# Graph network on one Trainium2 core: the aggregation passes gather each edge tile once instead of once per step

## What is computed

```python
def _sage_layer(h, edge_src, edge_dst, W, b, inv_deg):
    msgs = h[edge_src]
    agg = jax.ops.segment_sum(msgs, edge_dst, num_segments=h.shape[0]) * inv_deg
    y = jnp.concatenate([h, agg], axis=1)
    return y @ W + b
h = jnp.maximum(_layernorm(x, axis=-1), 0.0)
x = x + _L0_gnn_ref(h, src, dst, ...)     # two sage layers, relu between, log_softmax
h = jnp.maximum(_layernorm(x, axis=-1), 0.0)
x = x + _L1_gnn_ref(h, edge_index, edge_weight1, ...)   # two transformer convolutions
```

## Time and profile before

| | |
|---|---|
| median of 3 runs | 9773.23 us (9768.02 to 9782.53) |
| the profiled execution | 9781.53 us |
| its span from first to last instruction | 9779.8 us |
| GpSimd busy | 6426.5 us (66%) |
| VectorE busy | 5351.2 us (55%) |
| TensorE busy (matmul) | 5061.4 us (52%) |
| TensorE weight loads | 4259.1 us (44%) |
| ScalarE busy | 2964.1 us (30%) |
| line 537, first pass | 1664 gathers, 1595.2 us busy |
| line 537, second pass | 1664 gathers, 1581.2 us busy |
| line 1150, gathers of the convolution | 3328, 3187.6 us busy |

### The profile page before, as it was taken

How to read it: one execution, slowest core, us unless ns; L and a number is a source line. 1 busy time by engine, 2 the same in 40 slices (tenths; PEclk the granted TensorE clock), 3 DMA queues, 4 the chain that set the end, 5 groups by cost and what they waited for, 6 DMA issues and landing times. The chain is left out here.

```text
span 9779.8 us, 124105 instructions
## 1 busy us (share of the span) xinstructions
PE 5061.4 (52%) x23048; PEld 4259.1 (44%) x23048; DVE 5351.2 (55%) x14932; ACT 2964.1 (30%) x6482; POOL 6426.5 (66%) x6729
## 2 busy tenths in 40 slices
PE   1444444446544444443256666666655666666665
PEld 1333333335433333333145555555524555555553
DVE  5333333332333333333767777777766777777776
ACT  2000000001000000000236666666533666666653
POOL 4777777772577777776057777777605777777760
PEclk8555555557655555555677777777777777777777
DMA  5222222222222222222355555555435555555543
GB/s 119 53 53 53 53 53 53 53 53 71 67 53 53 53 53 52 53 53 55 97 173 163 162 162 162 162 162 163 145 104 170 165 164 163 162 163 163 162 145 106
DMA packets 601097, 1056.72 MB, mean 108 GB/s; under 512 B 213270, under 2 KB 371638, under 8 KB 600520
## 3 DMA queue, kind: packets, MB, share of 16 engines
q0 software_dynamic: 268320, 659.00, 24.2%
q1 hardware_dynamic: 238920, 323.21, 10.7%
q10 hardware_dynamic: 93408, 70.66, 2.3%
HBM read 974.79 MB, written 77.54 MB: 108 GB/s over the span
## 5 line engine op out<-in xcount | busy, mean ns | idle before, releaser
L1150 POOL DMA_INDIRECT conv_kv<-key_value,conv_src x3328 | 3187.6, 958 | 1714.1 <-issue 974.0
L537 POOL DMA_INDIRECT second_msg<-sage_hidden_projected,second_src x1664 | 1581.2, 950 | 748.5 <-issue 506.6
L537 POOL DMA_INDIRECT first_msg<-sage_in,first_src x1664 | 1595.2, 959 | 559.1 <-issue 506.8
L1371 PE MATMUL conv_ps_sums<-conv_kv,conv_sel 128*128 128x136 f32 x6656 | 1299.8, 347 | 531.2 <-DVE sums L1299 479.2
L594 PE MATMUL first_ps_sums<-first_msg,first_sel 128*128 128x129 f32 x3328 | 856.6, 438 | 1269.1 <-DVE first_sel L548 801.1
L594 PE MATMUL second_ps_sums<-second_msg,second_sel 128*128 128x129 f32 x3328 | 857.1, 438 | 1245.8 <-DVE second_sel L548 953.0
L1357 PE MATMUL conv_ps_query<-query_table,conv_selT 128*128 x6656 | 1353.1, 367 | 279.0 <-issue 151.5
L1371 PEld LDWEIGHTS conv_ps_sums<-conv_kv,conv_sel 128*128 128x128 f32 x6656 | 1124.5, 244 | 672.9 <-DVE sums L1299 658.0
L1357 PEld LDWEIGHTS conv_ps_query<-query_table,conv_selT 128*128 128x128 f32 x6656 | 1188.8, 265 | 367.4 <-issue 353.1
L594 PEld LDWEIGHTS first_ps_sums<-first_msg,first_sel 128*128 128x128 f32 x3328 | 744.5, 329 | 1381.1 <-DVE first_sel L548 880.9
L594 PEld LDWEIGHTS second_ps_sums<-second_msg,second_sel 128*128 128x128 f32 x3328 | 745.1, 329 | 1358.0 <-DVE second_sel L548 1015.7
(11 more groups left out here) (211 smaller groups left out, 4581.3 us busy)
## 6 DMA issues: line engine op xcount, KB each, us to landing
conv_place<-place_rows SPq DMA_DIRECT2D x416, 512.0 KB
conv_kv<-key_value,conv_src POOLq DMA_INDIRECT x3328, 3.6
first_msg<-sage_in,first_src POOLq DMA_INDIRECT x1664, 2.5
second_msg<-sage_hidden_projected,second_src POOLq DMA_INDIRECT x1664, 2.5
key_value<-project_kv ACTq DMA_DIRECT2D x28, 896.0 KB
conv_pen<-run_penalties SPq DMA_DIRECT2D x416, 48.5 KB
project_hT<-conv_in_transposed SPq DMA_DIRECT2D x28, 448.0 KB
combine_hT<-conv_in_transposed SPq DMA_DIRECT2D x28, 448.0 KB
```

The lines of the kernel that those rows point to most:

```text
L537: pool.indirect_dma_start(msg[:, (b % 2) * CH + j, 0:D], None, table, bass.IndirectOffsetOnAxis(ap=src[:, b, j:j + 1], axis=0)).then_inc(g ...
L1150: pool.indirect_dma_start(kv[:, h * CH + j, :], None, t.kv_d, bass.IndirectOffsetOnAxis(ap=src[:, h, j:j + 1], axis=0)).then_inc(gathered[ ...
L1371: last = pe.matmul(sums_of(h, step), sel[:, k % SELG, step % GR, :], kv[:, h * CH + step, DEN:2 * D], start=True, stop=True)
```

## The change

`sage_edges` gathers each edge tile once, 391 groups of 4 tiles (TILES = 1564), and the steps read a tile where it lies in the ring of 64 places. Setup writes three new tables, each with one word for a step: the ring place of its tile, the group of its tile, and (by tile) the group of steps that reads the tile last. TensorE loads the places of 16 steps into registers and addresses `msg` with them; for every 8 steps it loads the tile group that they need and waits until so many groups have come. ScalarE waits for the 16 `gathered` semaphores in turn and raises one count, `tiles_in`. SyncE waits for the last use of each tile group and raises `place_free`, for which GpSimd waits. SyncE loads source columns of 64 tiles from a copy of the input laid out in columns by the host. The gathers themselves, the selections and VectorE's additions stay as they are. With the constants of this case RG = 16 groups of places, SB = 64, LAPS = 12 and REST = 7.

```diff
+TILES = -(-E // (P * GR)) * GR
+GROUPS = TILES // GR
+RG = RING // GR
+SB = RG * GR
+LAPS, REST = divmod(GROUPS, 2 * RG)
+EARLY = 8
...
-                    sp.wait_ge(steps_out, 64)
+                    for table, rows_i in ((t.slot_d, slot), (t.need_d, need), (t.last_d, lastuse)):
+                        sp.dma_start(table.rearrange("(j p) -> p j", p=P), rows_i[:, :],
+                                     allow_slow_non_contiguous=True).then_inc(steps_out, 16)
+                    sp.wait_ge(steps_out, 112)
...
                 link(dve.tensor_copy(ti[:, :], tf[:, :]))
+                link(dve.tensor_scalar(tcap[:, :], tf[:, :], TILES - 1.0, None, ALU.min))
+                link(dve.tensor_copy(tci[:, :], tcap[:, :]))
+                dve.tensor_scalar(slot[:, :], tci[:, :], RING - 1, None, ALU.bitwise_and)
+                dve.tensor_scalar(need[:, :], tci[:, :], GR.bit_length() - 1, None, ALU.arith_shift_right)
+                link(dve.tensor_copy(fini[:, :], fin[:, :]))
+                link(dve.tensor_scalar(lastuse[:, :], fini[:, :], GR.bit_length() - 1, None, ALU.arith_shift_right))
...
             @block.sync
             def _(sp):
...
+                def load_src(b, n):
+                    sp.dma_start(src[:, b, :], src_cols[:, bass.ds(n * SB, SB)]).then_inc(src_in[b], 16)
+
+                def release(n):
+                    last = sp.value_load(lastuse[0:1, bass.ds(n, 1)], min_val=0, max_val=STEPS // GR - 1)
+                    sp.wait_ge(sums_ready, last + 1)
+                    sp.sem_inc(place_free, 1)
+
+                load_src(0, 0)
+                load_src(1, 1)
+                sp.sem_inc(place_free, RG)
+                sp.dma_start(lastuse[:, :], t.last_d[0:TILES].rearrange("(a g e) -> a g e", a=1, e=GR)[:, :, GR - 1],
+                             allow_slow_non_contiguous=True).then_inc(last_in, 16)
+                sp.dma_start(rel[:, :], t.edge_d[:, 0, :]).then_inc(rel_in, 16)
+                sp.dma_start(slot[:, :], t.slot_d.rearrange("(a n) -> a n", a=1)).then_inc(slot_in, 16)
+                sp.dma_start(need[:, :], t.need_d.rearrange("(a g e) -> a g e", a=1, e=EARLY)[:, :, EARLY - 1],
+                             allow_slow_non_contiguous=True).then_inc(slot_in, 16)
+                sp.dma_start(blk[:, :], t.b_d.rearrange("(a c) t -> a (c t)", a=1)).then_inc(blk_in, 16)
+                sp.wait_ge(last_in, 16)
+                with sp.Fori(0, LAPS - 1) as g:
+                    for b in range(2):
+                        for k in range(RG):
+                            release(g * (2 * RG) + (b * RG + k))
+                        load_src(b, g * 2 + (b + 2))
...
             @block.gpsimd
             def _(pool):
...
-                            pool.wait_ge(sums_ready, KG * c + k + 1)
...
+                def gather(b, k, n, turn):
+                    pool.wait_ge(place_free, n)
+                    pool.sem_inc(go_p, 1)
+                    for i in range(GR):
+                        j = k * GR + i
+                        pool.indirect_dma_start(
+                            msg[:, j * MW:j * MW + D], None, table,
+                            bass.IndirectOffsetOnAxis(ap=src[:, b, j:j + 1], axis=0)).then_inc(gathered[k], 16)
...
+            @block.scalar
+            def _(act):
+                with act.Fori(0, 2 * LAPS) as g:
+                    for k in range(RG):
+                        act.wait_ge(gathered[k], 16 * GR * g + 16 * GR)
+                        act.sem_inc(tiles_in, 1)
...
             @block.tensor
             def _(pe):
...
+                        if k % (KG // 2) == 0:
+                            pe.load(regs, slot[0:1, bass.ds(g * (2 * CH) + (h * CH + k * GR), CH // 2)])
+                            at = [pe.snap(r, min_val=0, max_val=RING - 1) for r in regs]
+                        if k % (EARLY // GR) == 0:
+                            need_r = pe.value_load(need[0:1, bass.ds(g * (2 * CH // EARLY) + (h * CH + k * GR) // EARLY, 1)],
+                                                   min_val=0, max_val=GROUPS - 1)
+                            pe.wait_ge(tiles_in, need_r + 1)
...
+                            last = pe.matmul(ps[:, 2 * (k % 2) + i // 2, (i % 2) * MW:(i % 2) * MW + MW],
+                                             sel[:, place, :],
+                                             msg[:, bass.ds(at[(k * GR + i) % (CH // 2)] * MW, MW)], start=True, stop=True)
...
-    a.update(x=x, src=src, dst=dst, edge_weight1=wgt)
+    a.update(x=x, src=src, dst=dst, edge_weight1=wgt, src_cols=np.ascontiguousarray(src.reshape(STEPS, P).T))
```

More of the change, by code:

```diff
@@ L57 @@
 HK = 5
+TILES = -(-E // (P * GR)) * GR
[4 more added lines that the diff above has]
+EARLY = 8
+assert REST < RG and SB * (2 * LAPS + 1) <= STEPS
 assert NB % GB == 0 and NC_ % 2 == 0 and SJ * P == STEPS
@@ L178, in setup_phase @@
         bi = sb("bi", [P, SJ], I32)
+        tcap = sb("tcap", [P, SJ])
+        tci = sb("tci", [P, SJ], I32)
+        slot = sb("slot", [P, SJ], I32)
+        need = sb("need", [P, SJ], I32)
+        fini = sb("fini", [P, SJ], I32)
+        lastuse = sb("lastuse", [P, SJ], I32)
         b128 = sb("b128", [P, SJ])
@@ L489, in scalar, with sage_edges @@
             act.wait_ge(self.stored[h], 16 * (NG // 2) + 16)
-SRCB = 4
-assert NC_ % SRCB == 0
-def sage_edges(nc, t, table, tag):
+def sage_edges(nc, t, table, src_cols, tag):
     with room(nc, tag) as (sb, psum, sem):
-        msg = sb("msg", [P, RING, MW])
+        msg = sb("msg", [P, RING * MW])
         sel = sb("sel", [P, RING, P])
-        src = sb("src", [P, SRCB, CH], I32)
+        src = sb("src", [P, 2, SB], I32)
         rel = sb("rel", [P, STEPS])
         blk = sb("blk", [1, STEPS], I32)
+        slot = sb("slot", [1, STEPS], I32)
+        need = sb("need", [1, STEPS // EARLY], I32)
+        lastuse = sb("lastuse", [1, GROUPS], I32)
         ps = psum("ps_sums", [P, 4, 512])
-        ones_set, sums_set, rel_in, blk_in, go_v, go_p = (
-            sem(k) for k in ("ones_set", "sums_set", "rel_in", "blk_in", "go_v", "go_p"))
-        src_in = [sem(f"src_in{b}") for b in range(SRCB)]
-        gathered = [sem(f"gathered{k}") for k in range(2 * KG)]
-        sel_ready, sums_ready, ps_used, chain_v = (
-            sem(k) for k in ("sel_ready", "sums_ready", "ps_used", "chain_v"))
+        ones_set, sums_set, rel_in, blk_in, slot_in, last_in, go_p, go_v, go_t = (
+            sem(k) for k in ("ones_set", "sums_set", "rel_in", "blk_in", "slot_in", "last_in", "go_p", "go_v", "go_t"))
+        src_in = [sem(f"src_in{b}") for b in range(2)]
+        gathered = [sem(f"gathered{k}") for k in range(RG)]
+        place_free, tiles_in, sel_ready, sums_ready, ps_used, chain_v = (
+            sem(k) for k in ("place_free", "tiles_in", "sel_ready", "sums_ready", "ps_used", "chain_v"))
         with nc.Block() as block:
@@ L526, in _ @@
+                with sp.Fori(0, LAPS - 1) as g:
[4 more added lines that the diff above has]
+                for k in range(RG):
+                    release((LAPS - 1) * 2 * RG + k)
+                load_src(0, 2 * LAPS)
+                for k in range(REST):
+                    release((2 * LAPS - 1) * RG + k)
             @block.gpsimd
@@ new lines, in _ @@
+                with pool.Fori(0, LAPS) as g:
+                    for b in range(2):
+                        pool.wait_ge(src_in[b], 16 * g + 16)
+                        for k in range(RG):
+                            gather(b, k, g * (2 * RG) + (b * RG + k + 1), g)
+                pool.wait_ge(src_in[0], 16 * LAPS + 16)
+                for k in range(REST):
+                    gather(0, k, 2 * LAPS * RG + k + 1, LAPS)
+            @block.scalar
+            def _(act):
+                with act.Fori(0, 2 * LAPS) as g:
+                    for k in range(RG):
+                        act.wait_ge(gathered[k], 16 * GR * g + 16 * GR)
+                        act.sem_inc(tiles_in, 1)
+                for k in range(REST):
+                    act.wait_ge(gathered[k], 16 * GR * (2 * LAPS + 1))
+                    act.sem_inc(tiles_in, 1)
@@ L1776, in program @@
         declare_sums(nc, t, ctx)
-        sage_edges(nc, t, t.h_d, "first")
+        sage_edges(nc, t, t.h_d, a["src_cols"], "first")
         sage_dense(nc, t, a["L0_gnn_W1"], a["L0_gnn_b1"], a["L0_gnn_W2"], a["L0_gnn_b2"])
-        sage_edges(nc, t, t.p_d, "second")
+        sage_edges(nc, t, t.p_d, a["src_cols"], "second")
         sage_output(nc, t, a["L1_gnn_W_in"], a["L1_gnn_b_in"])
```

49 lines of the change are left out of this document (16 added, 33 removed).

## The result

The changed kernel takes 9521.69 us (median of 4 runs, 9517.16 to 9527.13), the kernel before 9772.11 us (4 runs, 9768.02 to 9782.53): a ratio of 0.9742, 95% interval 0.9726 to 0.9759. The forecast was 9531 us, 9515 to 9560. The profiled execution took 9527.13 us with a span of 9525.3, 254.5 us less than the span of before.

The account below looks back on a forecast made before the run. GpSimd's gathers, issued without pause, bound each pass: count times spacing. Gathers - 251.8, tails + 4.8 and setup + 5.2 give - 241.8 us, from the median 9773.2 to 9531 us; range 9515 to 9548 (80%), to 9560 (89%).

Parts of the forecast that it names:

- part 1: Passes: gathering each tile once drops 100 gathers a pass at the old spacings, saving 126.3 and 125.5 us, together 251.8.
- rival (e): Passes: the long gathers vanish with the new loop, 22 + 8 us less at most, 9501 to 9515 us; 2%.
- Part 2: Passes: GpSimd's new wait for place_free, raised by SyncE, has about 55 us to spare and costs 0.
- Part 3: Passes: TensorE's register loads and addresses, at most 24.6 us of a 37.7 us chunk with matmuls, cost 0.
- rival (b): Passes: hand-over through the ring partly on the path, for instance 39.5 us a chunk, losing 187 us: 9718 us; 5%.
- Part 4: Start and tail of a pass: later first sums cost 0, the tail grows 2.4 us a pass, 4.8 together.
- Part 5: Setup: six VectorE instructions add 1.2 us and three table writes make GpSimd wait 4, together 5.2 (2 to 15).
- (a): Setup: the norm, held up by scattered writes, ends after the gathers, adding 10 to 25 us: 9541 to 9556; 9%.
- (d): Passes: something other than the gather count sets the spacing per pass, nothing is saved, 9783 us; 1%.
- (c): Passes: TensorE and VectorE run strictly one after the other, 52.8 us a chunk, kernel 11063 us; 3%.

Follow-up runs that it names:

- e2: Changed kernel's hand-over, but each step given a tile of its own, so 1664 gathers a pass again; 9778.3 us, ratio 0.9999 to the old kernel.
- e1: Old kernel with only the change's six VectorE setup instructions and three table writes added, which nobody reads; 9772.6 us, ratio 0.9993 to the old kernel.
- e3: Changed kernel with SyncE reading tpi and tni back before writing the three new tables; 9524.0 us, ratio 0.9739 to the old kernel.
- e4: Old kernel with the three tables and their tiles declared but never written, on a second, slower chip; 12273.8 us, ratio 0.9998 to the old kernel there.
- e5: Changed kernel without edit on the second, slower chip; 12059.1 us, ratio 0.9827 to the old kernel there.
- e8: Changed kernel without edit on the third chip, also slower; 12253.2 us, ratio 0.9851 to the old kernel there.
- e9: Changed kernel with tpi and tni read back before the three tables are written, on the third chip; 12235.2 us, ratio 0.9841 to the old kernel there.
- e11: Changed kernel with TensorE loading its 16 registers anew ahead of each matmul, 32 times a chunk, on the third chip; 12895.8 us.

## Why the prediction was right

**The bound and part 1.** That a pass is its gathers times their spacing carried nearly all of the forecast, and e2 shows it: the same hand-over with 1664 gathers gives all 250 us back. 100 gathers were priced at 126.3 and 125.5 us; e2 against the changed kernel gives 127.6 and 127.4. The first pass gained 139.8 us instead of 126.3, and the term that was mis-sized is its spacing. It was 1.2635 and 1.2618 us in the two profiles of the old kernel, and 1.254 to 1.256 in e1, e2, e3 and the changed kernel. 1563 x (1.2635 - 1.2548) = 13.6 us is the whole of the surprise in that pass. I had carried the old spacing over; the outcome that the long gathers go was kept as rival (e), and some 14 of its 30 us came. The wide pass is the one that loads program code again and again (125 packets against 4 to 8 in every other pass on the first chip), and e1 and e4 together speak for the place of its instructions as the reason, and against that of its tables. So these 14 us are no merit of the change: e1 has them with the old passes. That the total still fell into the range is in part luck. The bounds that the prediction lists, with its 7 us for single runs, add up to 9520.5 to 9552.1 us and not to the 9515 to 9548 that it gives; 9521.7 lies at the very edge of them, since the 14 us were in no term of the sum and only some 3 us of dearer setup stood against them.

**Part 2, the hand-over through SyncE and ScalarE.** Taken at 0, and it was 0 on the first chip (e2). On the two slower chips GpSimd waits 274 to 313 us a pass for place_free, which the prediction had named as a sign against it: there the 0 isn't shown. The register load on SyncE, bounded by 0.1 and 1.11 us and put at 0.17, is 0.27 us, and a single one on TensorE 0.31 (min/median/max ns):

```profile
L543 SPq TENSOR_LOAD <-first_lastuse x375: 262/268/493, 193.9 to 2078.8; - x188
...
L651 PEldq TENSOR_LOAD <-first_need x208: 299/306/323, 200.0 to 2151.1; - x104
```

**Part 3, TensorE's registers.** 16 registers took 1.11 us as on the row of the convolution, and an address 46 ns. TensorE needs 16 + 2 x 1.1 + 4 x 0.3 + 1.5 = 21 us of the 37.7, as an estimate from these rows. The 28.2 us that the prediction gave VectorE left it 9.5 us idle, not the "over 10" that rival (b) counts on; measured, it was busy for 756.9 of 1961.3 us. The pause of VectorE at a chunk's start was up to 9.2 us in the old first pass and is at most 3.9 us in the new one, and it goes with the code loads, not with the change (e1).

**Part 4, start and tail.** The start of the sums moved from 26.0 us behind the first gather to 29.6 (220.33 against 190.7). That is 3.6 us more, a little under the 5 to 25 that were named, and it was hidden. The tail grew by 1.3 and 1.0 us instead of 2.4. The two groups of sums came as foreseen, and the hop through ScalarE is near the 0.35 us that it was put at: ScalarE raises its count at 2155.52 us and the first matmul starts at 2155.87 (VectorE frees its PSUM half at 2155.55, so the hop can't have been longer). What was left out is the time before the hop: TensorE starts 3.89 us after the start of the last gather, where it took 4.89. From there to the last sum it takes 1.9 us more than before, and from the last sum to the next stage 0.5 us more; less the 1.0 us ahead of it, that is the 1.3. Why the old kernel took 1 us longer from gather to matmul isn't shown.

```profile
2155.87 3.69 PE L659 MATMUL first_ps_sums<-first_msg,first_sel 128*128 x16 [2.21 <-DVEq L623]
2158.10 1.59 DVE L622 TENSOR_TENSOR sums<-sums,first_ps_sums 128x129 f32 x4 [2.59 <-PE first_ps_sums L659]
```

**Part 5, the setup.** Forecast + 5.2 us with bounds 2 and 15, measured + 8.4. The writes were done at 100.36 us, where 94.7 to 100.7 had been worked out, and GpSimd waited 6.77 us, what the dearer of the two prices gives (6.8), not the 4 that was taken between them. Other runs of the same writes ended at 94.3 (e2), 95.2 (e1), 97.1 (e5) and 103.0 us (e8), so no single price was to be had, and the forecast's two were the right kind of answer. The norm ended at 132.1 us, 22.4 later than before, within the 19 to 24 that had been worked out.

```profile
100.36 0.36 SPq L257 DMA_DIRECT2D setup_tpi<-tile_of_step  x1
...
105.25 0.94 POOL L280 DMA_INDIRECT setup_rows_prev<-in_dst,setup_tpi  x1 [6.77 <-DMA setup_tni<-tile_of_step]
...
132.11 0.17 DVE L440 SCALAR_TENSOR_TENSOR setup_ln_shift<-setup_ln_mean_var,setup_ln_rstd 128x7 f32<-128x7 f32 x1
...
139.10 1.03 DVE L325 CAST setup_df<-setup_rows_dst 128x1664 f32<-128x1664 int32 x1 [6.83 <-DMA setup_rows_next<-in_dst,setup_tni]
```

The fit in DMA: Bandwidth & Descriptors of the Trainium skill (Anatomy of one DMA), 2.0 us plus bytes over 436 GB/s, is given there for GpSimd's path and does not carry over to SyncE's scattered words: SyncE's near loads moved from 68.89 to 100.36 us for three tables of 6.7 KB, about 10 us for each, and to 94.3 in e2, about 8 for each.

**The rivals.** (a), a setup held up by the norm, did not come on the first chip, where it was 6.8 us away. On the slower chips the norm does end last (e4, e5, e8, e9), but the tables are not the cause: it ends at 168.5 us in e4, which writes none of them, and at 169.0 in e5, and the first gather comes at 219.5 and 219.9 us. (b), the hand-over on the path in part, is open on those chips. GpSimd waits for SyncE there, and the gain was 215 and 182 us instead of 250, but the old kernel waits too, and e2, which would part the hand-over's price from the rest, ran on the first chip alone. (d), nothing saved by fewer gathers, is refuted by e2 against the changed kernel. (c) never came, and e11 shows how much more work on TensorE it takes to lose the gain.

## What to carry to other kernels

When an engine that issues DMAs stands at 76% busy but has nothing named in front of the remaining 24%, take count times spacing as the time, and remove counts. Then test the new hand-over with the old count, as in e2: it parts the gain of the change from the price of its machinery in one run. When two passes of the same code have different spacings, count the packets of the instruction queues in each before carrying the wider one over. A margin that is comfortable in one profile (both engines had over 10 us a chunk idle) is a statement on that chip; price it by what the waits cost when each engine pauses now and then.

## What was not expected of the hardware

TensorE's granted clock in the passes rose from 0.50, the level of 1.2 GHz, to 0.60 and 0.63 on average, with the same matmuls in a somewhat shorter pass; its busy time fell from 854.5 to 762.7 and 751.0 us. e2 has the same matmuls and gathers as the old kernel and 0.58. What differs is that TensorE works on eight steps at a stretch and idles for 6 us, where it had worked on four and idled for 3. It changed nothing here, since TensorE wasn't the bound. On the slower chip the new kernel gets 0.53 and 0.54 in its passes (e5) and the old one 0.54 in both (e4), so the rise belongs to the first chip's rhythm and not to lots of eight as such.

Program code was loaded anew in lap after lap of one pass and not of the other: 125 packets of the instruction queue and 2101.1 us in the old first pass, 4 packets and 2085.8 us in e1 with the same code behind some added instructions, 124 packets in e4 without the added instructions. The trace links the packets to VectorE's 9 us pauses (four packets with each); their link to the longer gathers is that both come and go together.

On the two slower chips the sequencers' own instructions now and then take 0.7 or 1.4 us. On the first, such register and address instructions of the changed kernel have medians of 18 to 57 ns and never take over 0.23 us. This is VectorE's address arithmetic ahead of its additions, first in the changed kernel's profile, then in e8 (min/median/max ns):

```profile
L614 DVEq FUSED_REGOPS  x416: 60/223/226, 218.8 to 4334.9; - x139
...
L614 DVEq FUSED_REGOPS  x416: 2/226/1385, 247.5 to 5124.3; - x139
```

SyncE shows the same in both kernels. TensorE shows it in the new kernel alone: of its address, check and arithmetic instructions 270 take over 0.3 us in e5, none in e4. GpSimd shows none (68 ns at most in e4, 63 in e5). All that follows the passes, the convolution for the most part, was touched by no edit and takes some 7090 us there (e8) against 5157. What makes a chip do that isn't in these traces. The changed kernel runs 11000 more instructions (135116 against 124105 in all), most of them of this kind, so it has more to lose there, and the smaller gain agrees with it without proving it.
